# Attention's mask on GpSimd beside the row gathers in place of VectorE beside the last routed tiles

## The reference

```python
x = x + _L0_xattn_ref(_layernorm(x), token_ids, ctx, ctx, ctx)   # four experts chosen by token id
x = x + _L0_ffn_ref(_layernorm(x), ...)                          # 16 routed experts, 4 for each token, and a shared one
x = x + _L1_xattn_ref(_layernorm(x), ctx, seg_id, ...)           # 16 heads, masked by segment
x = x + _L1_ffn_ref(_layernorm(x), ...)                          # ternary weights, Hadamard transform
```

```python
k_ids = jnp.arange(lk)[None, None, :]
qs = seg_id[:, :, None]
good = (k_ids <= qs) & (k_ids >= qs - LOOKBACK)       # LOOKBACK = 8
scores = jnp.where(good[:, None, :, :], scores, NEG)
```

## Time and profile before

| | before |
| --- | --- |
| median of three runs | 605.02 us |
| lowest, highest | 602.88, 607.85 us |
| the profiled execution | 606.46 us |
| its span | 604.8 us |
| routed tiles: first turn of rows to the load of the kept keys | 145.00 to 265.43 us |
| GpSimd busy | 304.6 us, 297 instructions |

### The profile page before, as it was taken

How to read it: one execution, slowest core, us unless ns; L and a number is a source line. 1 busy time by engine, 2 the same in 40 slices (tenths; PEclk the granted TensorE clock), 3 DMA queues, 4 the chain that set the end, 5 groups by cost and what they waited for, 6 DMA issues and landing times.

```text
span 604.8 us, 11166 instructions
## 1 busy us (share of the span) xinstructions
PE 505.4 (84%) x3328; PEld 439.9 (73%) x3332; DVE 439.8 (73%) x1374; ACT 359.3 (59%) x902; POOL 304.6 (50%) x297
## 2 busy tenths in 40 slices
PE   0699978998889799973285999999999999588895
PEld 0588766877879788762265999899999998345673
DVE  4789947875866776967344777888888786759774
ACT  2344564343656668651035787888787888666543
POOL 2557751114433435205468899999776672252200
PEclk9999998999989899995575999999999999979996
DMA  7144443213545365477312111121000000000000
GB/s 265 55 119 149 141 131 113 67 44 100 144 132 175 105 186 111 117 243 229 83 28 32 22 20 27 18 29 18 10 2 2 2 2 2 0 1 1 18 27 26
DMA packets 30121, 45.25 MB, mean 75 GB/s; under 512 B 5680, under 2 KB 21904, under 8 KB 29424
## 3 DMA queue, kind: packets, MB, share of 16 engines
q1 hardware_dynamic: 20912, 28.15, 14.8%
q0 software_dynamic: 6096, 10.74, 9.2%
q10 hardware_dynamic: 3056, 5.65, 2.8%
HBM read 34.63 MB, written 8.85 MB: 72 GB/s over the span
## 4 chain that ended last, share of the span: by engine, by line
PE 36%; DVE 24%; issue 12%; POOL 11%; DMA 9%; ACT 6%; SPq 0%; POOLq 0%; DVEq 0%; ACTq 0%
PE bank L1079 6%; PE bank L413 6%; PE bank L414 5%; PE bank L415 5%; PE bank L1514 4%; POOL pr L639 3%; DMA X<-slots_y,slot 3%; DMA bw<-bits_dram 3%; POOL Q L652 2%; POOL Q L654 2%; DVE pT_lo L1573 2%; PE bank L1469 1%; ACT pr L955 1%; DVE X L1625 1%; DVE hn L1584 1%
## 5 line engine op out<-in xcount | busy, mean ns | idle before, releaser
L580 POOL DMA_INDIRECT inb<-rows_kept,row_of x47 | 47.0, 1001 | 49.0 <-PE bank L1079 35.1
L955 ACT ACTIVATE pr<-sc,smin 128x256 f32<-128x256 f32 x128 | 63.2, 500 | 0.0
L660 POOL TENSOR_TENSOR Q_lo<-Q,Q_hi 128x512 fp32r<-128x512 f32 x32 | 52.9, 1655 | 12.2 <-ACT Q_hi L695 12.2
L639 POOL TENSOR_TENSOR pr<-pr,srec 128x512 f32<-128x512 f32 x32 | 40.9, 1278 | 14.2 <-DVE srec L2075 14.1
L1573 DVE TENSOR_TENSOR pT_lo<-bank,pT_hi 128x512 fp32r<-128x512 f32 x64 | 41.1, 684 | 8.2 <-ACT pT_hi L695 8.2
L2068 DVE CUSTOM_DVE_ANT_0 sc<-bank,bias 128x256 f32<-128x256 f32 x128 | 46.5, 420 | 0.1
L695 ACT ACTIVATE pT_hi<-bank 128x512 fp32r<-128x512 f32 x64 | 34.9, 596 | 17.8 <-PE bank L1079 17.7
L1079 PE MATMUL bank<-const,pr 128*128 128x128 f32 x256 | 35.1, 281 | 7.8 <-POOL pr L639 7.6
L602 POOL DMA_INDIRECT X<-slots_y,slot x24 | 38.2, 1592 | 4.5 <-issue 3.8
L413 PE MATMUL bank<-K_hi,Q_hi 128*128 128x256 f32 x128 | 37.3, 291 | 3.0 <-POOL Q_lo L660 3.0
L538 POOL TENSOR_TENSOR Wd<-wd_raw,Wd 128x512 fp32r<-128x512 f32 x13 | 16.9, 1297 | 45.3 <-ACT Wd L742 45.2
(11 more groups left out here) (338 smaller groups left out, 1937.1 us busy)
## 6 DMA issues: line engine op xcount, KB each, us to landing
slots_y<-yb SPq DMA_DIRECT2D x47, 128.0 KB, 3.1
wg_raw<-gate_up_dram SPq DMA_DIRECT2D x22, 256.0 KB, 2.6
bw<-bits_dram ACTq DMA_DIRECT2D x3, 1024.0 KB, 7.9
wd_raw<-down_dram SPq DMA_DIRECT2D x16, 128.0 KB
wo<-wo_dram SPq DMA_DIRECT2D x2, 1024.0 KB, 6.6
wd_raw<-down_dram SPq DMA_DIRECT2D x30, 64.0 KB
gu_raw<-gate_up_dram SPq DMA_DIRECT2D x6, 256.0 KB, 3.3
X<-x_dram SPq DMA_DIRECT2D x2, 512.0 KB, 6.7
```

The costliest lines, as they stand in the source:

```text
L580: pool.indirect_dma_start(inb[:, j % NIN, :], None, rows_d, bass.IndirectOffsetOnAxis(row_of[:, j:j + 1], 0)).then_inc(slots_in[j % NIN], 16)
L639: pool.tensor_tensor(pr[:, r, 0:2, :], pr[:, r, 0:2, :], srec[:, r, 0:2].unsqueeze(2).to_broadcast([P, 2, S]), ALU.mult).then_inc(share_fi ...
L660: pool.tensor_tensor(Q_lo[:, i % 2, :], Q[:, i % 2, :], Q_hi[:, i % 2, :].bitcast(F32), ALU.subtract).then_inc(queries_low_g, 1)
L955: e = act.activation(pr[:, i % 2, z, :], sc[:, i % 2, z, :], ACT.Exp, bias=smin[:, i % 2, z:z + 1], scale=-1.0, accum_out=ssum[:, i % 2, z ...
```

## The change

The 24 mask operations (three for each of eight masks) move from VectorE to GpSimd. From gather 13 on, GpSimd issues one of them after each gather, until all are done after gather 36; the last stands before gather 37. A mask operation waits for the one before it (`mask_g`). The reductions over the partitions stay after gathers 12, 23 and 34, and where both follow one gather the mask operation comes first. SyncE's wait at tile 44 and a new wait of VectorE ahead of the first masked score are for all 24.

```diff
+        MASK = 13
...
-                    sp.wait_ge(mask_v, NT)
+                    sp.wait_ge(mask_g, 3 * NT)
...
+            def see(n):
+
+                t, step = divmod(n, 3)
+                if n:
+                    pool.wait_ge(mask_g, n)
+                if step == 0:
+                    pool.tensor_scalar(bias[:, t, :], keyix, segf[:, 0, t:t + 1], FAR, ALU.is_gt, ALU.mult).then_inc(mask_g, 1)
+                elif step == 1:
+                    pool.tensor_scalar(sbias[:, :], keyix, segf[:, 1, t:t + 1], FAR, ALU.is_lt, ALU.mult).then_inc(mask_g, 1)
+                else:
+                    pool.tensor_tensor(bias[:, t, :], bias[:, t, :], sbias[:, :], ALU.add).then_inc(mask_g, 1)
+
...
                 gather_slots(j)
+                if 0 <= j - MASK < 3 * NT:
+                    see(j - MASK)
                 if j - 8 in TERNARY:
                     i = TERNARY[j - 8]
                     pool.wait_ge(ternary_v, 3 * i + 1)
...
-            def see(t):
-
-                link(dve.tensor_scalar(bias[:, t, :], keyix, segf[:, 0, t:t + 1], FAR, ALU.is_gt, ALU.mult))
-                link(dve.tensor_scalar(sbias[:, :], keyix, segf[:, 1, t:t + 1], FAR, ALU.is_lt, ALU.mult))
-                dve.tensor_tensor(bias[:, t, :], bias[:, t, :], sbias[:, :], ALU.add).then_inc(mask_v, 1)
-                dve.wait_ge(mask_v, t + 1)
-
...
-                if j >= TILES - NT - 2 and j - (TILES - NT - 2) < NT:
-                    see(j - (TILES - NT - 2))
...
             def masked(i, h):
                 b_, r = i // NPAIR, i % 2
+                if i == 0 and h == 0:
+                    dve.wait_ge(mask_g, 3 * NT)
```

More of the change, by code:

```diff
@@ L287, in build @@
          hit_v, place_v, placed_p, slot_share_v, slots_turned_p, slots_high_a, slots_low_v, slots_gate_up_p, slots_silu_a, slots_hidden_v, hidden_turned_p,
-         turned_high_a, turned_low_v, slots_down_p, slots_copied_a, ternary_v, ternary_total_g, ternary_done_a, ternary_rounded_a, mask_v) = [sem(n) for n in (
+         turned_high_a, turned_low_v, slots_down_p, slots_copied_a, ternary_v, ternary_total_g, ternary_done_a, ternary_rounded_a, mask_g) = [sem(n) for n in (
              "routing_v logits_exp_a routing_p "
@@ L294, in build @@
              "ternary_v ternary_total_g ternary_done_a ternary_rounded_a "
-             "mask_v").split()]
+             "mask_g").split()]
         (compressed_p, compressed_high_a, compressed_low_v,
```

## The result

The changed kernel takes 630.78 us (629.42 to 631.46, 4 runs) against 605.57 (602.88 to 607.85, 4 runs): a ratio of 1.043 with a 95% interval of 1.038 to 1.048. The forecast was 612.9, in a range of 600 to 626: slower, as foretold, but by 25 us and not by 8. The profiled execution took 629.42 us with a span of 627.8; the one before took 606.46 with 604.8.

A forecast was written before the change was run, and what follows sets the result against it. The prediction saw no single engine bounding the whole: TensorE or VectorE paced the routed tiles, and GpSimd's queue would after the change. Terms of -4.5, +17.7, -6.3 and +1.0 gave +7.9, so 612.9 us, range 600 to 626.

The forecast's parts named there:

- Term 2: GpSimd's queue, gathers 13 to 36: gathers, masks, gaps, reductions and five loads sum to 75.9 us; tile 36 late, +17.7 us.
- Term 1: Routed tiles: without masks on VectorE, the last tiles run at TensorE's step of 1.99 us, -4.5 us.
- rival 4: GpSimd's masks: heavy compare operations of 1.52 us each, +14.7 us, 627.6 us in all; chance 0.13.
- Term 3: After the tiles: the code load at 283.9 goes, so power and the first tile's `hn` end sooner, -6.3 us.
- Term 4: TensorE after its wait at tile 36: a stretch at 1.2 and not 2.4 GHz, +1.0 us.
- rival 1: GpSimd's queue: masks need no code load after a reduction, leaving only Term 1, 600.5 us; chance 0.07.
- rival 2: GpSimd's queue: short loads, up to 3.1 us each, hide, so the kernel is faster, -10.8, 594.2 us; chance 0.06.
- Rival 3: GpSimd's masks: light compare operations of 0.34 us, as on VectorE, 4.2 less, 608.7 us; chance 0.22.
- Costed at nothing: Mask-to-mask, SyncE and VectorE waits, and VectorE's `picked` held up by GpSimd up to 0.76 us, in idle time: 0 us.

The follow-up runs named there:

- run 4: Kernel before plus 21 extra operations at the end of GpSimd's stream, seven forms three times each, to time compares and adds: 604.49 us (one execution).
- run 5: Changed kernel with an add in place of each compare in the masks, so the masks hold other numbers: 619.37 us, ratio 1.025.
- Run 10: Changed kernel with four `yb` buffers in place of three: 630.12 us, ratio 1.040.
- Run 7: Kernel before with one 128x1 add on GpSimd after its last gather of the tiles, to bring the code load forward: 601.31 us, ratio 0.992.
- run 2: Changed kernel without the three reductions over the partitions, so GpSimd's masks need no code change: 594.44 us, ratio 0.984.
- run 1: Kernel before, masks on VectorE, with a 128x1 add on GpSimd behind gathers 13, 24 and 35 to force code loads: 616.55 us, ratio 1.019.
- run 11: Changed kernel with the 24 masks on GpSimd moved from beside the row gathers to its wait for stores and later: 601.78 us, ratio 0.995.

## Why the prediction was right or wrong

The direction and the mechanism were right: the source view of the queue, five more loads, tiles late in the order foretold, the load at 283.9 gone. The size was wrong, by one term above all.

- **Term 2** was mis-sized. Gather 13 to gather 36 takes 262.22 - 172.30 = 89.9 us, not 75.9, in the same parts: gathers 24.2 in place of 22.1 (1.05 us each beside masks, not 0.95); mask operations 23.6 in place of 14.9 (16 x 1.15 + 7 x 0.74); loads 34.65 in place of 33.1; gaps and reductions 7.5 in place of 5.8. That is 14.0 us more, of which 8.7 are the masks. With a landing of 3.0 and not 3.9 us, tile 36 is 31.2 us late (forecast 17.7). The failed step is "I take 0.6, nearest to the add, since it reads one input and not two"; runs 4 and 5 put 1.15 in its place and show that the difference comes back almost whole in the time. Alone it would have made 621.6 us, still inside the range; what carried the time past 626 is that the smaller misses lie on the same side too: gathers 2.1, gaps 1.7, loads 1.6 and, below, term 1's 2.4. The upper bound of 1.52 held, and it was dismissed with too little: rival 4 stood at 0.13, and the range left half of it out.
- **Term 1** was right in the turns: tiles 40 to 46 take 287.77 - 275.78 = 12.0 us and not 15.3, -3.3. The 1.2 us more at the end did not come. From tile 46's turn to the first load of the kept keys it is 8.2 us (287.8 to 296.0) against 7.0 before (258.5 to 265.4): faster tiles meet their own stores behind the next layer's loads. "What is late next" was not asked of the stores. Run 10 shows that wait shrink with one more buffer: there the same stretch takes 5.5 us (290.16 to 295.64).
- **Term 3** was right in this kernel: the first `hn` ends at 318.92, 24.1 us later than before (294.83), while the gathers of `yk` start 30.6 later (303.22 against 272.64): -6.5 against a forecast of -6.3. Run 7 has this part alone: 2.4 us by the medians, 0.5 to 1.2% (3 to 7 us) by the interval of its ratio, and only 22.2 - 19.5 = 2.7 in its trace. So the size hangs on when the rows of `yk`'s second group land, which the sum took as fixed; that they landed as before in the changed kernel was luck, not foresight.
- **Term 4** was about right: tiles 36 to 40 take 10.6 us in place of 9.2, +1.4; in the 2 us after tile 36's wait the granted clock is 0.50, that is 1.2 GHz. How much of the 1.4 is the clock was not separated.
- The sum from the trace is 31.2 + 1.4 - 3.3 + 1.2 - 6.5 = +24.0 us, against 23.0 of span.
- **Rivals 1 to 3** fell: seven pairs and not three (1); loads of 5.9 to 7.8 us (2); compares three times as dear as on VectorE (3). Rival 3 had leaned on the Trainium skill, "GPSIMD Engine Reference", section 4.1 "Engine selection", by which one-input work runs near VectorE's rate; here an add of this form, 0.48 us against VectorE's 0.34 for the compare, comes nearest to that, and a compare at 1.16 does not.
- **Costed at nothing**: two compares of run 2 took 2.18 and 1.97 us while VectorE clipped 2048 columns (1.22 and 1.32 us), in place of 1.15. The reverse of the expected harm, GpSimd held up by VectorE, but only twice. The Trainium skill, "SBUF — State Buffer", section "Who interferes with whom", describes a port pair that the two share with an exclusive lock, held by whoever issues first. The delays of 1.03 and 0.82 us fit a lock; the order does not in the first case, where the compare had started first (178.83 against 179.54) and was delayed all the same.

## What to carry to other kernels

Idle time on an in-order engine is worth what its queue lets through. Before handing work to GpSimd, look at its own queue in the trace for code changes, order the work so that kinds of code do not alternate, and count the whole queue up to the next instruction that somebody waits for; slack used once by new work no longer hides what it hid before. Price an operation that the trace does not show by both bounds, and let the range reach them: a compare is not an add. And a load that cannot be avoided can be brought forward into a wait by one tiny operation (run 7).

## What the runs showed of the hardware that was not expected

- On GpSimd, 128x256 f32 with one input: add and multiply 0.48 us, multiply 0.87, compare and multiply 1.16, compare alone 1.34 (run 4). The form with fewer steps is not the cheaper one.
- The way back from the reduction to elementwise code takes 6.9 to 8.1 us (runs 1, 5, 7, 11 and the changed kernel), the way to the reduction 5.9 to 6.4 where nothing else covers it; gathers run under either.
- The same edit can cost nothing, 10 us or 25: loads alone +10.5, masks alone no loss (-3 to -4.4, inside the noise), both +25.
